# A relation layer's row-fetching matmuls cut into seven pieces and dealt out between the thin stages of a step

## The chip, the cores and the metric

The kernel runs on one core of a Trainium2 chip. What counts is the device time of one launch in microseconds, the median of several runs. A separate execution is taken by the hardware profiler; its times are in the profile.

## The reference

A graph of 6250 nodes with 128 features and 200,000 edges goes through two layers of weighted neighbour means with a normalised output, a residual and a layer norm, and then through one relation layer (32 relations in 8 bases) with a residual and a layer norm. The change touches the relation layer alone:

```python
def _L1_gnn_ref(h, src, dst, etype, norm, weight, w_comp, bias_param):
    hsrc = h[src]
    coef = w_comp[etype]
    msg = jnp.zeros((hsrc.shape[0], weight.shape[2]), dtype=h.dtype)
    for b in range(weight.shape[0]):
        msg = msg + hsrc @ weight[b] * coef[:, b][:, None]
    msg = msg * norm
    node_repr = jax.ops.segment_sum(msg, dst, num_segments=h.shape[0])
    node_repr = node_repr + bias_param
    return jax.nn.relu(node_repr)

x = _layernorm(x + _L0_gnn_ref(x, edge_index, edge_weight, L0_gnn_W1, L0_gnn_b1, L0_gnn_W2, L0_gnn_b2), axis=-1)
x = _layernorm(x + _L1_gnn_ref(x, src, dst, edge_type_32, edge_weight1, L1_gnn_weight, L1_gnn_w_comp, L1_gnn_bias_param), axis=-1)
```

## The kernel before

The kernel builds a dense adjacency matrix in DRAM, streams it twice for the two layers of means, and ends with the relation layer, which fills the span from about 2080 us on. Edges come in tiles of 128, ordered by destination. The first 428 tiles are sorted again by source into 7 classes of 7 node blocks (CLASS_BLOCKS = 7), and their source rows are fetched on TensorE; the other 1140 tiles' rows are gathered by GpSimd with indirect DMAs.

The layer runs in 114 steps (STEPS), the first 112 of which (GROUPS) have a group of four sorted tiles beside ten gathered ones. All semaphores and the order of every engine are written out by hand. In step s, TensorE has these parts:

- `tiles_summed(s, i)` (L1310): five gathered tiles, each one matmul of 128 rows by 64 columns (8 bases by 8 nodes). A step has two such halves.
- `sources(i, part)` (L1284): 21 matmuls of 512 columns in bf16 that fetch the rows of four sorted tiles. Each of 7 node blocks has three (high, middle and low part of the rows), all accumulated in PSUM bank 2. SOURCE_PARTS cuts them into three parts of 9, 6 and 6. The one-hot matrix ST2 comes from VectorE (L1749). ScalarE copies bank 2 into GT (`sources_copied`, L995); the next group's first part waits for that copy (s_gc).
- `sources_turned(i)` (L1319): four transposes of GT, which ScalarE copies into G2 (`turned_copied`, L1002).
- `wide_summed(i, c)` (L1327): one matmul of 336 columns for each of the four sorted tiles, from G2 and the matrix C2 (L1741).
- `coefficients(s)` (L1266, L1270): one and three small matmuls from the relation one-hot matrices, which ScalarE makes (`relations`, L972 to L981) from relation numbers that SyncE spreads over the partitions (`types_spread`, L624 and L629). They write bank 7. ScalarE copies them into COEF (`coefficients_copied`, L989); VectorE makes the matrices C (L1728) and C2 of them.
- `block_multiplied(n)` (L1346): for a node block whose sums are complete, eight matmuls with the bases' weights into another part of bank 7. ScalarE takes the result (`block_taken`, L1021) and clears that part of the ring of sums (L1026). 46 steps have one product, or two.
- `result_transposed(m)` (L1357): for four finished node blocks. VectorE adds the residual and normalises (L1806 to L1822); SyncE stores (`stored`, L644).

VectorE adds every matmul's output to rings of sums in SBUF: L1769 for each gathered tile, L1778 for each sorted one, at positions that it loads into registers between two steps (L1753). Its order in a step is: first half's additions, matrix C of the next step, results, two wide additions, one-hot matrix of step s + 3, matrix C2, joins, two wide additions, second half's additions.

The outputs of tiles, wide matmuls, transposes and results go round a ring of six PSUM banks. UNITS lists them in the order of their making, and `unit_bank_free(n)` waits for the reader of the unit six places before.

In the kernel before, TensorE's order in step s is: tiles, first half; sources of s + 2, part 0; two wide matmuls; sources, part 1; products; two wide matmuls; tiles, second half; sources, part 2; coefficients of s + 2; transposes of s + 1; results. ScalarE's is: products and results taken; copies of the fetched rows of s + 2, of the coefficients of s + 2, of the transposes of s + 1; relations of s + 3.

SyncE issues the loads for step s in one loop, and waits in it for a result's normalisation before it stores the result.

Of the kernel before, what the change touches and what calls it, by code (L numbers as in the profile page):

```python
# [44 lines left out]
CLASSES = 7  # L45
# [43 lines left out]
UNIT_BANKS = [0, 1, 3, 4, 5, 6]  # L89
RING_BANKS = len(UNIT_BANKS)  # L90
KEPT_CHUNK = 10
SOURCE_PARTS = [(0, 3), (3, 5), (5, CLASS_BLOCKS)]


def sorted_begun(r):
# [71 lines left out]
for step in range(STEPS):  # L167
    if step == 0:
        UNITS.append((0, "turn", 0))
    UNITS.append((step, "tile", 0))  # L170
    if step < GROUPS:
        UNITS += [(step, "wide", i) for i in range(PER)]
    UNITS.append((step, "tile", 1))
    if step + 1 < GROUPS:
        UNITS.append((step + 1, "turn", 0))
    UNITS += [(step, "result", m) for m in range(len(OUT_AT)) if OUT_AT[m] == step]
UNITS += [(step, "result", m) for step in range(STEPS, OUT_AT[-1] + 1) for m in range(len(OUT_AT)) if OUT_AT[m] == step]
UNIT = {u: n for n, u in enumerate(UNITS)}
# [57 lines left out]
def regular(nc, flag, x, src, dst, etype, w, w1, lin1, b1, lin2, b2, Wrel, wcomp, brel, out):  # L236
    with ExitStack() as ctx:
# [563 lines left out]
        def _(act):  # L801
# [242 lines left out]
            for s in range(OUT_AT[-1] + 3):  # L1044
                if KEPT_CHUNK + s < len(CHUNKS):
                    halved(KEPT_CHUNK + s)
                for n in events_in(s - 1):
                    block_taken(n)
                for m in range(len(OUT_ORDER)):
                    if OUT_AT[m] == s - 1:  # L1050
                        rooted(m)
                if s + 2 < GROUPS:
                    sources_copied(s + 2)
                if s + 2 < STEPS:
                    coefficients_copied(s + 2)
                if s + 1 < GROUPS:
                    turned_copied(s + 1)
                if s + 3 < STEPS:
                    relations(s + 3)

        @block.tensor
        def _(pe):
# [195 lines left out]
            def coefficients(s):  # L1258
                pe.wait_ge(s_rel, marked_to(s))
                if s:  # L1260
                    pe.wait_ge(s_coefc, s)
                before = events_to(s - 3, lambda n: True)
                if before:
                    product_taken(before - 1)
                if s < GROUPS:
                    nc.tensor.matmul(bank(7, PER * BASES, STEP_TILES * BASES), RELT2[s % 2],  # L1266
                                     wcd[0:PER * RELS, 0:PER, :].rearrange("p a b -> p (a b)"), start=True, stop=True)
                for q in range(-(-STEP_TILES // 4)):
                    k = min(4, STEP_TILES - 4 * q)
                    last = nc.tensor.matmul(bank(7, k * BASES, q * 4 * BASES), RELT[s % 2][0:k * RELS, q * P:(q + 1) * P],  # L1270
                                            wcd[0:k * RELS, 0:k, :].rearrange("p a b -> p (a b)"), start=True, stop=True)
                last.then_inc(s_coef, 1)

            def sources(i, part):
                if part == 0:
                    pe.wait_ge(s_st2, i + 1)
                    if i:
                        pe.wait_ge(s_gc, i)
                first = group_of(i) // ROUNDS_SORTED * CLASS_BLOCKS
                begin, end = SOURCE_PARTS[part]  # L1280
                pe.wait_ge(s_low, CHUNK_OF[first + end - 1] + 1)
                for j in range(begin, end):
                    for a, rows_part in enumerate((XS[:, first + j, 0, :], XS[:, first + j, 1, :], LOW[:, first + j, :])):
                        last = nc.tensor.matmul(bank(2), rows_part, ST2[i % 2][:, j, :],  # L1284
                                                start=(j == 0 and a == 0), stop=(j == CLASS_BLOCKS - 1 and a == 2))
                if end == CLASS_BLOCKS:
                    last.then_inc(s_gs, 1)

            def unit_bank_free(n):
# [48 lines left out]
            def block_multiplied(n):  # L1338

                step, ring, b = EVENTS[n]  # L1340
                pe.wait_ge(s_addg if ring == "gathered" else s_adds, added_after(step, ring))
                pe.wait_ge(s_coefc, min(step + 3, STEPS))
                if n:
                    product_taken(n - 1)
                for a in range(BASES):
# [16 lines left out]
            coefficients(0)  # L1362
            coefficients(1)
            for i in range(2):
                for part in range(len(SOURCE_PARTS)):
                    sources(i, part)
                if i == 0:
                    sources_turned(0)
            pe.wait_ge(s_zero, 2)
            for s in range(OUT_AT[-1] + 1):  # L1370
                if s < STEPS:
                    tiles_summed(s, 0)
                if s + 2 < GROUPS:
                    sources(s + 2, 0)
                if s < GROUPS:
                    wide_summed(s, 0)
                    wide_summed(s, 1)
                if s + 2 < GROUPS:
                    sources(s + 2, 1)
                for n in events_in(s - 1):  # L1380
                    block_multiplied(n)
                if s < GROUPS:
                    wide_summed(s, 2)
                    wide_summed(s, 3)
                if s < STEPS:
                    tiles_summed(s, 1)
                if s + 2 < GROUPS:
                    sources(s + 2, 2)
                if s + 2 < STEPS:
                    coefficients(s + 2)  # L1390
                if s + 1 < GROUPS:
                    sources_turned(s + 1)
                for m in range(len(OUT_ORDER)):
                    if OUT_AT[m] == s:
                        result_transposed(m)
# [1639 lines left out]
```

## Time and profile before

| | us |
|---|---|
| median of 3 runs | 3764.12 |
| lowest and highest run | 3760.8, 3773.42 |
| span of the profiled execution | 3868.7 |

The profiled execution is another one than the three timed runs; its span goes from the first to the last instruction. On its page, TensorE's matmuls are busy for 3418.3 us (88%), VectorE for 2465.0 (64%), GpSimd for 2415.7 (62%) and ScalarE for 1351.6 (35%). The granted TensorE clock, in tenths over forty slices, is 9 in most of the first half and 8 in nearly all of the relation layer:

```profile
PEclk6999999999999999999998889888888888888897
```

In the views, PE is TensorE's matmuls, PEld its weight loads, DVE VectorE, ACT ScalarE, POOL GpSimd and SP SyncE. L1284 is line 1284 of the kernel. A float32 matmul stands as two records. The ends of matmuls are modelled, so neighbouring ones overlap, and the distance between starts is the better measure. "Remote" and "issue" as the end of a wait mean that the profile finds no instruction that ended it.

### The profile page before, as it was taken

To read this page: it belongs to the slowest core of one execution; us is meant where nothing else is said; L and a number is where in the kernel's file an instruction comes from. 1 tells how busy PE (TensorE), PEld (TensorE's weight loads), DVE (VectorE), ACT (ScalarE), POOL (GpSimd) and SP (SyncE) were. 2 spreads that over 40 slices of the span, in tenths; PEclk is the share of its full clock that TensorE was granted. 3 is DMA by queue.
4 is the path that set the end of the run, shared out by engine and by line. 5 is a ranking of instruction groups with operands and counts; after the bars stand their busy time and mean duration, and the time that the engine had idled before them with its cause. 6 is when DMAs were issued, how large, how long until landed. Compare 5 with 4: busy or idle time off the path is not lost.

```text
span 3868.7 us, 52705 instructions
## 1 busy us (share of the span) xinstructions
PE 3418.3 (88%) x17077; PEld 2281.2 (59%) x17077; DVE 2465.0 (64%) x4684; ACT 1351.6 (35%) x3452; POOL 2415.7 (62%) x2636
## 2 busy tenths in 40 slices
PE   3999999998999999999996888888988888988885
PEld 3899999984533344544443555556655556655554
DVE  7999999995776663022033666666656666666664
ACT  5999999990000000010002222222222222222221
POOL 5888888880036775555523666666666666666663
PEclk6999999999999999999998889888888888888897
DMA  6677777778779999999993222232222222222222
GB/s 185 192 206 205 206 208 208 208 205 291 263 233 256 269 259 269 301 271 275 293 298 93 65 66 70 60 78 70 70 57 71 65 74 67 73 65 69 67 66 46
DMA packets 532789, 618.45 MB, mean 160 GB/s; under 512 B 74011, under 2 KB 460127, under 8 KB 532399
## 3 DMA queue, kind: packets, MB, share of 16 engines
q1 hardware_dynamic: 478895, 528.52, 46.9%
q0 software_dynamic: 53616, 86.51, 8.9%
q8 instruction: 140, 2.29, 0.2%
q14 instruction: 138, 1.13, 0.1%
HBM read 445.83 MB, written 168.99 MB: 159 GB/s over the span
## 4 chain that ended last, share of the span: by engine, by line
PE 49%; ACT 19%; DVE 8%; issue 8%; DMA 7%; another core or an unknown queue 7%; DVEq 2%; POOL 1%; SPq 0%; ACTq 0%; POOLq 0%
PE PS L1231 21%; ACT arena L845 11%; PE PS L1284 10%; DMA arena<-adjacency 7%; ACT arena L861 6%; PE PS L1310 5%; PE PS L1327 5%; PE PS L1270 2%; PE PS L1119 2%; PE PS L1346 1%; DVE XT L1769 1%; PE PS L1319 1%; DVEq L1753 1%; DVE H L1749 1%
## 5 line engine op out<-in xcount | busy, mean ns | idle before, releaser
L797 POOL DMA_INDIRECT arena<-x_table,rec x1140 | 1159.6, 1017 | 613.0 <-issue 309.8
L776 POOL DMA_INDIRECT sorted_records<-arena x428 | 505.9, 1182 | 556.2 <-PE PS L1231 476.5
L1119 PE MATMUL PS<-arena 128*98 128x128 f32 x6272 | 761.6, 279 | 46.3 <-DVE arena L1508 13.0
L1119 PEld LDWEIGHTS PS<-arena 128*98 128x98 f32 x6272 | 708.4, 166 | 95.9 <-issue 50.4
L733 POOL TENSOR_SCALAR arena<-iota,H,arena 128x98 f32<-128x98 f32 x980 | 674.2, 702 | 91.7 <-PE PS L1119 89.2
L1284 PE MATMUL PS<-H,X 128*128 128x512 bf16 x1568 | 548.9, 436 | 74.5 <-issue 66.9
L845 ACT ACTIVATE arena<-arena 128x98 f32<-128x98 f32 x1568 | 582.9, 686 | 12.7 <-DVE arena L1506 12.6
L1231 PE MATMUL PS<-arena,X 128*128 128x512 f32 (+1 forms) x1274 | 541.4, 577 | 39.3 <-DMA arena<-adjacency 38.6
L1231 PE MATMUL PS<-arena,H 128*128 128x512 f32 (+1 forms) x1274 | 527.8, 570 | 16.0 <-DMA arena<-adjacency 15.5
L861 ACT ACTIVATE arena<-PS 98x1024 f32<-98x1024 f32 x392 | 519.6, 1325 | 12.5 <-PE PS L1119 12.5
L1769 DVE TENSOR_TENSOR XT<-XT,PS 128x64 f32 x1140 | 252.1, 221 | 421.6 <-issue 188.8
L1508 DVE TENSOR_TENSOR arena<-PS,H 128x2048 f32<-128x2048 f32 x196 | 447.0, 2280 | 0.0
L1687 DVE TENSOR_TENSOR arena<-arena 128x1536 f32<-128x1536 f32 (+1 forms) x192 | 343.9, 1791 | 157.2 <-DMA arena<-adjacency 151.5
L1231 PEld LDWEIGHTS PS<-arena,X 128*128 128x128 f32 x1274 | 237.4, 192 | 322.4 <-issue 193.3
L1231 PEld LDWEIGHTS PS<-arena,H 128*128 128x128 f32 x1274 | 238.5, 190 | 293.8 <-issue 215.3
L1310 PEld LDWEIGHTS PS<-arena 128*128 128x128 f32 x2280 | 320.6, 213 | 78.9 <-issue 46.8
L1310 PE MATMUL PS<-arena 128*128 128x64 f32 x2280 | 323.3, 292 | 46.5 <-issue 33.4
L1327 PE MATMUL PS<-arena 128*128 128x336 f32 x896 | 313.5, 472 | 43.5 <-issue 35.5
L1284 PE MATMUL PS<-H,arena 128*128 128x512 bf16 x784 | 337.6, 431 | 1.2 <-issue 1.0
L1778 DVE TENSOR_TENSOR arena<-arena,PS 128x336 f32 x448 | 224.7, 501 | 173.9 <-remote 75.7
L1284 PEld LDWEIGHTS PS<-H,X 128*128 128x128 bf16 x1568 | 172.5, 117 | 257.4 <-issue 162.9
L995 ACT ACTIVATE rec<-PS 128x512 f32<-128x512 f32 x112 | 66.7, 596 | 682.7 <-remote 439.7
(259 smaller groups left out, 3139.6 us busy)
## 6 DMA issues: line engine op xcount, KB each, us to landing
arena<-adjacency SPq DMA_DIRECT2D x294, 768.0 KB
adjacency<-arena SPq DMA_DIRECT2D x196, 784.0 KB
arena<-adjacency SPq DMA_DIRECT2D x98, 832.0 KB
arena<-x_table,rec POOLq DMA_INDIRECT x1140
XT<-sorted_source_rows SPq DMA_DIRECT2D x112, 128.0 KB
arena<-in_edge_type SPq DMA_DIRECT2D x226, 48.0 KB
arena<-in_edge_type SPq DMA_DIRECT2D x226, 32.0 KB
XT<-sorted_relations SPq DMA_DIRECT2D x448, 8.0 KB
```

The costliest lines, as they stand in the source:

```text
L733: last = nc.gpsimd.tensor_scalar(S1[:, r, :], iota[:, 0:M1], K1T[:, v:v + 1], WWT[:, v:v + 1], ALU.is_equal, ALU.mult)
L776: pool.indirect_dma_start(rec2_d, bass.IndirectOffsetOnAxis(ap=SLOT[:, t:t + 1], axis=0), R4[:, t, :], None).then_inc(s_scat, 16)
L797: pool.indirect_dma_start(G[:, n % HELD_UNITS * UNIT_TILES + i, :], None, x1_d, bass.IndirectOffsetOnAxis(ap=SRC[:, t:t + 1], axis=0)).the ...
L845: nc.scalar.activation(S1[:, r, :], S1[:, r, :], ACT.Copy, scale=WWT[:, v:v + 1]).then_inc(s_wa, 1)
L861: nc.scalar.activation(ST[0:M1, n % 3, q * GROUP * P:(q + 1) * GROUP * P], PS[0:M1, q * GROUP * P:(q + 1) * GROUP * P], ACT.Copy).then_inc ...
L1119: last = nc.tensor.matmul(bank(2 * q + j // 4, P, j % 4 * P)[0:M1, :], S1[:, r, :], S2[:, r, :], start=True, stop=True)
L1231: last = nc.tensor.matmul(bank(bank0 + c, nb * P), (X, H1)[l][:, k, :], AB[n % 4][:, off:off + nb * P], start=(k == 0), stop=(k == NBLK - 1))
L1284: last = nc.tensor.matmul(bank(2), rows_part, ST2[i % 2][:, j, :], start=(j == 0 and a == 0), stop=(j == CLASS_BLOCKS - 1 and a == 2))
L1310: last = nc.tensor.matmul(bank(UNIT_BANKS[n % RING_BANKS], BASIS, j * BASIS), G[:, half % HELD_UNITS * UNIT_TILES + j, :], C[s % 2][:, fir ...
L1327: nc.tensor.matmul(bank(UNIT_BANKS[n % RING_BANKS], WIDE_BASIS), G2[i % 2][:, c, :], C2[i % 2][:, c, :, :].rearrange("p b j -> p (b j)"), ...
L1508: nc.vector.tensor_tensor(S2[:, whole, :], bank(4, P).unsqueeze(1).to_broadcast([P, BATCH, P]), each(K2T, n).to_broadcast([P, BATCH, P]), ...
L1687: nc.vector.tensor_tensor(ACC[p % 2][:, 0:width], ACC[p % 2][:, 0:width], AB[n % 4][:, 0:width], ALU.add).then_inc(s_acc, 1)
```

## The change

TensorE fetches a group's rows in seven pieces of three matmuls, one for each node block, where it had three parts of 9, 6 and 6. In step s the order becomes: tiles, first half; piece 0; transposes of s + 1; piece 1; two wide matmuls; piece 2; coefficients of s + 2; piece 3; products; two wide matmuls; piece 4; tiles, second half; pieces 5 and 6; results.

ScalarE's order becomes: transposes of s + 1, relations of s + 3, coefficients of s + 2, products and results taken, fetched rows of s + 2.

In the list of units, the transposes stand behind the first half of tiles and no longer behind the second. Two waits follow the new order. The coefficients wait for the products up to those of four steps before their own index, instead of three. A product waits for the copy of one more step's coefficients. The wait for the low part of the rows (s_low) is made for each piece, in the first seven groups only.

```diff
-SOURCE_PARTS = [(0, 3), (3, 5), (5, CLASS_BLOCKS)]
@@
     UNITS.append((step, "tile", 0))
+    if step + 1 < GROUPS:
+        UNITS.append((step + 1, "turn", 0))
     if step < GROUPS:
         UNITS += [(step, "wide", i) for i in range(PER)]
     UNITS.append((step, "tile", 1))
-    if step + 1 < GROUPS:
-        UNITS.append((step + 1, "turn", 0))
@@ scalar
                 if KEPT_CHUNK + s < len(CHUNKS):
                     halved(KEPT_CHUNK + s)
+                if s + 1 < GROUPS:
+                    turned_copied(s + 1)
+                if s + 3 < STEPS:
+                    relations(s + 3)
+                if s + 2 < STEPS:
+                    coefficients_copied(s + 2)
                 for n in events_in(s - 1):
                     block_taken(n)
...
                 if s + 2 < GROUPS:
                     sources_copied(s + 2)
-                if s + 2 < STEPS:
-                    coefficients_copied(s + 2)
-                if s + 1 < GROUPS:
-                    turned_copied(s + 1)
-                if s + 3 < STEPS:
-                    relations(s + 3)
@@ coefficients
-                before = events_to(s - 3, lambda n: True)
+                before = events_to(s - 4, lambda n: True)
@@ sources
-            def sources(i, part):
-                if part == 0:
+            def sources(i, j):
+                first = group_of(i) // ROUNDS_SORTED * CLASS_BLOCKS
+                if j == 0:
                     pe.wait_ge(s_st2, i + 1)
                     if i:
                         pe.wait_ge(s_gc, i)
-                first = group_of(i) // ROUNDS_SORTED * CLASS_BLOCKS
-                begin, end = SOURCE_PARTS[part]
-                pe.wait_ge(s_low, CHUNK_OF[first + end - 1] + 1)
-                for j in range(begin, end):
-                    for a, rows_part in enumerate((XS[:, first + j, 0, :], XS[:, first + j, 1, :], LOW[:, first + j, :])):
-                        last = nc.tensor.matmul(bank(2), rows_part, ST2[i % 2][:, j, :],
-                                                start=(j == 0 and a == 0), stop=(j == CLASS_BLOCKS - 1 and a == 2))
-                if end == CLASS_BLOCKS:
+                if i < CLASSES:
+                    pe.wait_ge(s_low, CHUNK_OF[first + j] + 1)
+                for a, rows_part in enumerate((XS[:, first + j, 0, :], XS[:, first + j, 1, :], LOW[:, first + j, :])):
+                    last = nc.tensor.matmul(bank(2), rows_part, ST2[i % 2][:, j, :],
+                                            start=(j == 0 and a == 0), stop=(j == CLASS_BLOCKS - 1 and a == 2))
+                if j == CLASS_BLOCKS - 1:
                     last.then_inc(s_gs, 1)
@@ block_multiplied
-                pe.wait_ge(s_coefc, min(step + 3, STEPS))
+                pe.wait_ge(s_coefc, min(step + 4, STEPS))
@@ the loop over steps
+                ahead = s + 2 < GROUPS
                 if s < STEPS:
                     tiles_summed(s, 0)
-                if s + 2 < GROUPS:
+                if ahead:
                     sources(s + 2, 0)
+                if s + 1 < GROUPS:
+                    sources_turned(s + 1)
+                if ahead:
+                    sources(s + 2, 1)
                 if s < GROUPS:
                     wide_summed(s, 0)
                     wide_summed(s, 1)
-                if s + 2 < GROUPS:
-                    sources(s + 2, 1)
+                if ahead:
+                    sources(s + 2, 2)
+                if s + 2 < STEPS:
+                    coefficients(s + 2)
+                if ahead:
+                    sources(s + 2, 3)
                 for n in events_in(s - 1):
                     block_multiplied(n)
                 if s < GROUPS:
                     wide_summed(s, 2)
                     wide_summed(s, 3)
+                if ahead:
+                    sources(s + 2, 4)
                 if s < STEPS:
                     tiles_summed(s, 1)
-                if s + 2 < GROUPS:
-                    sources(s + 2, 2)
-                if s + 2 < STEPS:
-                    coefficients(s + 2)
-                if s + 1 < GROUPS:
-                    sources_turned(s + 1)
+                if ahead:
+                    sources(s + 2, 5)
+                    sources(s + 2, 6)
```

## Rows read from the trace of the kernel before

**Rows 1.** The page's first line.

```profile
span 3868.7 us, 52705 instructions
```

**Rows 2.** By windows: length, each engine's busy us and instructions, granted clock, DMA share, GB/s.

```profile
2110.00:3760.00 1650.00, 1426.03 (x7334) 972.33 (x7333) 1060.57 (x3151) 431.61 (x1067) 1091.06 (x1073) 0.87 0.26 68
```

**Rows 3.** Timeline of VectorE, step 60: start, us, line, count, idle time before.

```profile
3018.00 1.64 DVE L1769 TENSOR_TENSOR XT<-XT,PS 128x64 f32 x5 [2.79 <-issue]
...
3027.22 1.64 DVE L1769 TENSOR_TENSOR XT<-XT,PS 128x64 f32 x5
3031.06 0.93 DVE L1769 TENSOR_TENSOR XT<-XT,PS 128x64 f32 x3 [2.20 <-issue]
```

**Rows 4.** Waits of VectorE, 2110 to 3760 us: total us, times, longest.

```profile
DVE XT L1769 <- issue: 179.5, 79, 2.8
DVE arena L1778 <- remote: 72.5, 28, 6.7
...
DVE arena L1778 <- ACT arena L1026: 18.1, 7, 4.9
```

**Rows 5.** Timeline of TensorE, step 60 and the start of step 61.

```profile
3027.17 1.23 PE L1310 MATMUL PS<-arena 128*128 128x64 f32 x10
3028.23 0.59 PE L1284 MATMUL PS<-H,X 128*128 128x512 bf16 x2
...
3030.18 1.29 PE L1327 MATMUL PS<-arena 128*128 128x336 f32 x4
...
3033.73 1.22 PE L1310 MATMUL PS<-arena 128*128 128x64 f32 x10
...
3036.09 0.30 PE L1266 MATMUL PS<-wcd,XT 128*128 128x32 f32 x2
...
3037.09 0.66 PE L1319 MATMUL PS<-ident,rec 128*128 128x128 f32 x4
3037.58 0.56 PE L1310 MATMUL PS<-arena 128*128 128x64 f32 x2
```

**Rows 6.** Timeline of ScalarE, 3013 to 3019 us.

```profile
3013.63 0.60 ACT L995 ACTIVATE rec<-PS 128x512 f32<-128x512 f32 x1 [15.34 <-remote]
...
3016.49 0.51 ACT L972 ACTIVATE H<-arena,rel_of 128x256 f32<-128x256 int32 x1
...
3018.32 0.39 ACT L981 ACTIVATE XT<-XT,ones 128x128 f32<-128x128 f32 x1
```

**Rows 7.** Timeline of TensorE, 3006 to 3016 us.

```profile
3006.69 0.38 PE L1284 MATMUL PS<-H,arena 128*128 128x512 bf16 x1
...
3014.32 1.01 PE L1284 MATMUL PS<-H,X 128*128 128x512 bf16 x2 [4.70 <-issue]
...
3015.56 1.06 PE L1284 MATMUL PS<-H,X 128*128 128x512 bf16 x2
```

**Rows 8.** Waits of all engines, 2100 to 3790 us: ScalarE's longest.

```profile
ACT rec L995 <- remote: 439.7, 47, 17.9
```

**Rows 9.** By windows: a stretch of thin matmuls and the one behind it.

```profile
2157.70:2161.10 3.40, 2.74 (x21) 2.30 (x20) 3.15 (x10) 0.00 (x0) 2.49 (x4) 1.00 0.19 47
2161.10:2174.80 13.70, 7.18 (x16) 2.80 (x17) 8.00 (x24) 3.41 (x9) 9.23 (x9) 0.50 0.21 54
```

**Rows 10.** Waits of TensorE, 2110 to 3760 us.

```profile
PE PS L1266 <- ACT H L1021: 14.3, 7, 3.1
```

**Rows 11.** Timelines of TensorE and SyncE: the first and the last of nine such steps.

```profile
2514.17 1.00 PE L1310 MATMUL PS<-arena 128*128 128x64 f32 x8
2519.07 1.84 SPq L629 DMA_DIRECT2D arena<-in_edge_type  x4
...
3685.82 1.23 PE L1310 MATMUL PS<-arena 128*128 128x64 f32 x10
3692.64 1.84 SPq L629 DMA_DIRECT2D arena<-in_edge_type  x4
```

More of the change, by code:

```diff
@@ L1364, in _ @@
             for i in range(2):
-                for part in range(len(SOURCE_PARTS)):
-                    sources(i, part)
+                for j in range(CLASS_BLOCKS):
+                    sources(i, j)
                 if i == 0:
```

## The prediction

> **What bounds the kernel now.** I read the page first, then the relation stage by itself, then one step of it on each engine, and last what each engine waits for. The page gives the span [rows 1]; the change touches only its last stage. The view by windows [rows 2] has that stage's steps 0 to 106 between 2110 and 3760 us, 107 steps in 1650 us: 15.4 us a step. TensorE's granted clock is 0.87 there: it was at its lower level, 1.2 GHz, for 26% of the time (1 - 0.26/2 = 0.87).
>
> VectorE next. In a step in which it waits for nobody, its first tile addition starts at 3018.00 and that of the next step at 3031.06 [rows 3]: 13.06 us. Some 2.2 to 2.8 us of these are shown as idle "issue"; there it loads the ring positions for the next step's additions (L1753) into registers, which no engine can shorten. What VectorE loses to others is in its waits [rows 4]. The gaps ahead of L1769 are nearly all these loads (179.5 us in 79). Ahead of L1778 stand 72.5 us of waits for a late signal of TensorE and 18.1 for a ring that ScalarE clears. With the smaller groups of the same kind, and 20 us beyond the loads ahead of L1769, I count 137 us of true waits. So VectorE has (1650 - 137)/107 = 14.1 us of its own in a mean step (13.06, and about 1 for joins, wraps and the ten results).
>
> TensorE has less. Step 60 at the full clock [rows 5] runs from 3027.17 to 3037.58: 10.4 us. By its starts: five tiles 1.06; nine row-fetching matmuls 1.95 (0.65 for three); four wide ones with six fetching ones between them 3.55 (3.55 - 1.30 = 2.25, 1.13 for two); tiles and six fetching ones 2.36; coefficients 1.00; transposes 0.49. A block product (46 steps have them, four of these have two) adds about 2, so 11.4 on average at the full clock and 11.4/0.87 = 13.1 at the clock it got. That is under VectorE's 14.1. **VectorE sets the period**; TensorE runs ahead of it (tiles of step 60 at 3027.17, their addition at 3031.06: 3.9 us; in other steps up to 10) and matters only when it falls behind.
>
> **The profiled execution is longer than the others.** Its span is 3868.7 us, the median of the runs 3764.12: 104.6 less. I ask where the 105 us are, because they decide what can be gained. ScalarE, idle for 15.34 us, begins the copy of step 58's fetched rows at 3013.63 [rows 6], but the last matmul that it waits for stands at 3006.69 to 3007.07 [rows 7]: the completion was told 6.5 us late. TensorE's next fetch waits for that copy, so it starts at 3014.32, and the clock has fallen: three fetching matmuls take 1.24 us instead of 0.65. ScalarE's waits for such signals with nothing to match them come to 439.7 us in 47 of 112 copies [rows 8]. If that happens only under the profiler, about 105 of VectorE's 137 us of waits aren't there in an ordinary run, and 32 us are left for any change of TensorE's order.
> The Trainium skill (NOTIFIC — the notification-queue block, section 7.1) says that the recorder's internal pipeline holds back its producers when it is full. By that rule the late signals are the profiler's; no run here shows it, and no number below needs it.
>
> **The change part by part.**
> 1. Order. Matmuls, banks, copies are the same in number; nothing is added or removed but waits that are already met (one on s_low for each piece of the first seven groups). Counted from the step's start by the pieces of [rows 5]: tiles 0 to 1.06, piece 1.71, transposes 2.20, piece 2.85, two wide 3.98, piece 4.63, coefficients 5.63, piece 6.28, products, two wide 7.41, piece 8.06, tiles 9.12, two pieces 10.4. The same 10.4: zero.
> 2. Clock. Before, coefficients, transposes, and the next tiles lie side by side, 2.6 us with few columns. A fall is seen behind such a place: 2157.7 to 2161.1 has TensorE busy for 2.74 of 3.40 us, mostly with thin matmuls, at the full clock, and the 13.7 us after it are at 1.2 GHz [rows 9]. Spread out, no thin group but the tiles is over 1.1 us long. If half the low-clock time went (430 us of the stage's 1650, half of it lost), TensorE would gain some 105 us. It isn't on the path: VectorE's own 14.1 us hide it, and of the 32 us of waits I give it 15.
> The Trainium skill (TensorE: Matmul & The Clock Gate, "The HAM clock gate") has the clock go back to half when the engine stands idle and return with activity. That leaves open what thin work counts for, and a TensorE with 3 us to spare in 14 will stand idle somewhere in any order; by that rule this part is worth about nothing.
> 3. Coefficients. They no longer wait for the product of the same step to be taken (the bound moves from s - 3 to s - 4): L1266 <- ACT L1021, 14.3 us in 7 waits [rows 10], and the likes, 23 us in all. TensorE again, so 5 us of VectorE's waits.
> 4. Products. They now stand behind the coefficients and a piece: at 6.28 instead of 1.06 + 1.95 + 1.13 + 1.29 = 5.43, 0.85 us later. VectorE's third wide addition waits for the ring that ScalarE clears after them: 18.1 us in 7 waits [rows 4], 25 in 12 with the second ring. 12 x 0.85 = 10 us worse.
> 5. A new wait: a product writes bank 7 and must find coefficients s + 2 copied. ScalarE does this behind the transposes' copy and the relations of s + 3, six activations from 3016.49 to 3018.71 [rows 6], 2.2 us: 2.20 + 0.6 + 2.2 = 5.0, before the coefficients end at 5.63; the copy is done by 6.0, before 6.28. Zero, if the relation numbers are there. In nine steps they aren't: SyncE has just waited for a result. First such step: tiles at 2514.17, the last load issued until 2520.91; last: 3685.82 and 3694.48 [rows 11], 8.7 us into the step, and landing is later still. Then relations until 10.9, coefficients' copy until 11.2, against 6.28: TensorE stands 4.9 us or more if the step has a product (five of the nine). Queued behind: products, wide matmuls, tiles, the fetches; on ScalarE the clearing and the next copy of fetched rows. TensorE's lead of 4 to 10 us covers this; the charge is 0 at one end and 5 x 5 + 4 x 2 = 33 at the other (2 where there is no product, for the late copy of fetched rows); I take 4, as the lead is longer in most steps.
> 6. Fetched rows. The next step's first piece waits for their copy. Before, coefficients, transposes and tiles (2.55 us) lay between; now the tiles alone (1.06), against 0.38 - 0.22 + 0.60 and hops, about 0.85. Zero with 0.2 to spare at the full clock; if the signals are late in ordinary runs too, up to 1.5 us a step of TensorE, under its cover.
> 7. Banks. The ring of six now makes the second tiles wait for the first tiles' additions of the same step: ready at 3031.06 + 1.64 in step 60, 5.5 us into the step, against 8.06; where TensorE leads by 10 it waits 3.6 us. VectorE needs these tiles only 9.2 us after its first addition began (3027.22 against 3018.00), so this shortens the lead and costs nothing by itself.
> Sum: -15 - 5 + 10 + 4 = -6; with VectorE's own time untouched. Bounds: below, all 32 us; above, +15.
>
> **The rivals.**
> A. VectorE's waits are real in ordinary runs, and the steadier clock ends them. For it: late signals fit no copy's length, and nothing here proves them to be the profiler's. Then the sum is taken from 137: two fifths of it, 55, less the 10 of part 4: -45, 3719 us; at most -100.
> B. Slower: ScalarE's relations, now ahead of the coefficients and the fetched rows' copy, hold TensorE in the nine steps behind a late SyncE, just where results already eat its lead. It decides from where the lead is under 4.9 us: step 60's is 3.9. With 33 us for that, 10 for the products, less 20 gained: +23, 3787 us.
> C. It doesn't do what it says: the clock falls from idle time, not from thin work, and stays 0.87; parts 3 to 5 cancel: 3764 us.
>
> **How the numbers follow.** Forecast: VectorE-bound, a small gain, 45%: 3764.1 - 6 = 3758 us, range 3732 to 3779. A 23%, B 20%, C 12%. This kernel's measurement can tell 0.3%, 11 us, from no change. Faster: a third of the forecast (0.15) and all of A (0.23), 0.38. Slower: B (0.20) and 0.03 from the upper end of the forecast, 0.23. Same: 0.39. The range takes in most of A and B: 3700 to 3800; beyond lie a quarter of A (100 us is its most) and a fifth of B, whose signals may be late too (part 6).
>
> **What would show it.** In the profile after: DVE L1769's start to start still 13.1 us in quiet steps and 15 on average (forecast), under 14.6 (A). Clock of the stage: 0.90 or more (part 2), 0.87 (C). ACT L989 idle, ended by something late, ahead of PE L1346 in steps 27, 52, 65, 81, 91 (B). PE L1310 waiting for DVE L1769 (part 7), L1266 no more for ACT L1021 (part 3). I am wrong if VectorE's own operations get shorter in runs without the profiler, or if the first piece of a step waits for ScalarE throughout.

## The result, and the profile after

The changed kernel takes 3781.59 us (3775.89 to 3789.68, six runs), the kernel before 3764.03 in the same comparison: 17.6 us longer, ratio 1.0041, interval 1.0025 to 1.0057. I had forecast 3758 us and a small gain. The time lies in the range of 3700 to 3800, but it moved the other way, as rival B has it.

The page of the changed kernel begins with its span, which is now that of an ordinary run (its own time is 3789.68); the span of before was 105 us over its timed runs [rows 1]:

```profile
span 3787.9 us, 52562 instructions
```

The view by windows, 2110 to 3760 us (columns as in [rows 2]), has the layer's clock at 0.93. The 0.87 of before belongs to an execution with late signals, so the two can't be set against each other as they stand:

```profile
2110.00:3760.00 1650.00, 1386.89 (x7592) 973.85 (x7732) 1127.85 (x3363) 471.99 (x1156) 1185.11 (x1140) 0.93 0.30 73
```

VectorE's waits, 2110 to 3690 us (line, who ended it, total us, times, longest):

```profile
DVE XT L1775 <- issue: 130.6, 54, 2.8
DVE XT L1775 <- PE PS L1325: 120.9, 47, 3.1
DVE arena L1784 <- DVE arena L1784: 42.6, 194, 0.6
...
DVE arena L1784 <- ACT XT L1025: 6.7, 5, 2.8
DVE XT L1775 <- PE PS L1308: 5.9, 6, 1.3
DVE arena L1784 <- ACT arena L1025: 5.1, 1, 5.1
```

L1775 and L1784 are the additions that were L1769 and L1778. The first two rows are the register loads, 2.5 us each, whatever ended a wait in them; the third is VectorE behind itself. The waits for late signals, 72.5 us ahead of L1778 alone [rows 4], are gone altogether, though not by the change, as the experiments show. What is left are waits of 1 to 5 us, and they lie in six steps, found by going through the additions in order: 27 (4.2 us), 52 (1.9), 65 (1.1), 78 (3.7), 81 (1.3) and 91 (5.4), 17.6 in sum. These are the five steps with a product behind a late load that the prediction names (steps 27, 52, 65, 81, 91), and step 78, whose product I had overlooked. The trace has ten late loads, not nine; the other four, in steps 39, 45, 103 and 108, have no product behind them and cost VectorE nothing.

Step 91 shows how. SyncE, then ScalarE, TensorE and VectorE:

```profile
3445.72 0.41 SPq L643 DMA_DIRECT2D out<-H  x1
...
3448.66 1.90 SPq L628 DMA_DIRECT2D arena<-in_edge_type  x4
```

```profile
3452.86 0.51 ACT L971 ACTIVATE arena<-arena,rel_of 128x256 f32<-128x256 int32 x1 [9.16 <-DMA arena<-in_edge_type]
...
3454.98 0.24 ACT L988 ACTIVATE XT<-PS 128x112 f32<-128x112 f32 x1
```

```profile
3439.60 1.22 PE L1308 MATMUL PS<-arena 128*128 128x64 f32 x10
...
3449.40 1.10 PE L1269 MATMUL PS<-wcd,H 128*128 128x32 f32 x6
...
3455.32 3.75 PE L1344 MATMUL PS<-XT,Wr 128*128 128x128 f32 x16 [4.07 <-issue]
3459.63 3.75 PE L1344 MATMUL PS<-arena,Wr 128*128 128x128 f32 x16 [0.55 <-ACT H L1020]
```

```profile
3451.58 1.64 DVE L1775 TENSOR_TENSOR XT<-XT,PS 128x64 f32 x5 [2.81 <-issue]
...
3464.87 0.50 DVE L1784 TENSOR_TENSOR arena<-arena,PS 128x336 f32 x1 [5.13 <-ACT arena L1025]
```

SyncE stores a result at 3445.72, once VectorE has normalised it, and only then asks for the relation numbers (3448.66). ScalarE waits 9.16 us for them, makes the relations, and behind them the copy of the coefficients (L988, 3454.98), though those had been multiplied since 3450.5. The products (L1344) wait for that copy and are both slow, and the ring that ScalarE clears after them (L1025) is 5.13 us late for VectorE's third wide addition. TensorE began the step 12.0 us ahead of VectorE (3439.60 against 3451.58), and it didn't help.

Half of what a product takes here is the clock. A product that didn't have to wait takes 1.95 us, as in step 88 of the same trace; by windows (the last three numbers are granted clock, DMA share and GB/s), it has the full clock and the two of step 91 have half of it:

```profile
3403.35 1.95 PE L1344 MATMUL PS<-XT,Wr 128*128 128x128 f32 x16
```

```profile
3403.40:3405.30 1.90, 1.90 (x18) 1.90 (x17) 0.34 (x2) 0.00 (x0) 1.59 (x2) 1.00 0.29 73
3455.40:3463.30 7.90, 7.35 (x33) 7.08 (x34) 4.27 (x11) 1.31 (x2) 0.00 (x0) 0.50 0.20 49
```

All seven products of the six steps ran like this, at 0.50 and in 3.75 us each. TensorE had stood idle for 3.5 to 6.5 us before the first of each step.

### The profile page after: what moved, and what is told of

It is laid out like the page before. It is cut to its first block, busy times and chain, and to the rows that moved or that the text cites. A ratio compares the mean times of both kernels' runs of the same rounds, so it can differ in the third digit from the quotient of the medians.

```text
span 3787.9 us, 52562 instructions
## 1 busy us (share of the span) xinstructions
PE 3315.4 (88%) x16935; PEld 2226.6 (59%) x17077; DVE 2466.3 (65%) x4684; ACT 1361.5 (36%) x3452; POOL 2442.2 (64%) x2636
## 4 chain that ended last, share of the span: by engine, by line
PE 33%; DVE 21%; ACT 18%; DMA 11%; issue 9%; DVEq 7%; POOL 1%; SPq 0%; POOLq 0%; ACTq 0%
PE PS L1230 19%; ACT arena L844 11%; DMA arena<-adjacency 10%; ACT arena L860 6%; DVE XT L1775 5%; DVEq L1759 5%; DVE H L1755 5%; PE PS L1282 3%; PE PS L1325 2%; DVE arena L1784 2%; PE PS L1308 2%; PE PS L1344 2%; PE PS L1118 2%; DVEq L1775 1%; DVE arena L1734 1%
## 5 line engine op out<-in xcount | busy, mean ns | idle before, releaser
L796 POOL DMA_INDIRECT arena<-x_table,rec x1140 | 1185.1, 1040 | 458.2 <-issue 329.7
L1230 PE MATMUL PS<-arena,H 128*128 128x512 f32 (+1 forms) x1274 | 535.5, 575 | 31.2 <-DMA arena<-adjacency 30.9
L860 ACT ACTIVATE arena<-PS 98x1024 f32<-98x1024 f32 x392 | 520.2, 1327 | 12.3 <-PE PS L1118 12.3
L1775 DVE TENSOR_TENSOR XT<-XT,PS 128x64 f32 x1140 | 252.0, 221 | 407.8 <-issue 137.0
L1282 PE MATMUL PS<-H,X 128*128 128x512 bf16 x1447 | 461.6, 395 | 62.4 <-DVE H L1755 52.6
L1308 PEld LDWEIGHTS PS<-arena 128*128 128x128 f32 x2280 | 304.2, 203 | 110.4 <-DVE XT L1775 83.8
L1308 PE MATMUL PS<-arena 128*128 128x64 f32 x2280 | 301.9, 283 | 59.8 <-DVE XT L1775 58.8
L1282 PE MATMUL PS<-H,arena 128*128 128x512 bf16 x763 | 300.9, 394 | 0.4 <-issue 0.4
L1512 DVE TENSOR_TENSOR arena<-PS,H 128x1078 f32<-128x1078 f32 x196 | 250.6, 1279 | 41.4 <-PE PS L1118 34.2
L1325 PEld LDWEIGHTS PS<-arena 128*128 128x128 f32 x896 | 165.6, 199 | 185.9 <-issue 67.7
L1784 DVE TENSOR_TENSOR arena<-arena,PS 128x336 f32 x448 | 224.3, 501 | 68.7 <-DVE arena L1784 44.9
```

The lines of the kernel that those rows point to most:

```text
L796: pool.indirect_dma_start(G[:, n % HELD_UNITS * UNIT_TILES + i, :], None, x1_d, bass.IndirectOffsetOnAxis(ap=SRC[:, t:t + 1], axis=0)).the ...
L860: nc.scalar.activation(ST[0:M1, n % 3, q * GROUP * P:(q + 1) * GROUP * P], PS[0:M1, q * GROUP * P:(q + 1) * GROUP * P], ACT.Copy).then_inc ...
L1230: last = nc.tensor.matmul(bank(bank0 + c, nb * P), (X, H1)[l][:, k, :], AB[n % 4][:, off:off + nb * P], start=(k == 0), stop=(k == NBLK - 1))
L1308: last = nc.tensor.matmul(bank(UNIT_BANKS[n % RING_BANKS], BASIS, j * BASIS), G[:, half % HELD_UNITS * UNIT_TILES + j, :], C[s % 2][:, fir ...
L1325: nc.tensor.matmul(bank(UNIT_BANKS[n % RING_BANKS], WIDE_BASIS), G2[i % 2][:, c, :], C2[i % 2][:, c, :, :].rearrange("p b j -> p (b j)"), ...
L1775: nc.vector.tensor_tensor(a, a, bank(UNIT_BANKS[n % RING_BANKS], BASIS, j * BASIS).rearrange("p (b j) -> p b j", j=SPAN), ALU.add).then_in ...
```

## The experiments

Theories ahead of the first runs: 1, late relation numbers are the whole difference; 2, a small loss in every step; 3, it lies before the layer. Each edit was measured beside the kernel before on the same chip, and the comparisons turned out to be of two kinds: in some TensorE's signals come on time, in others late. So ratios and not times are to be compared. Four comparisons, on three chips, had late signals; one chip came up twice, late both times (3859.8 and 3886.2 us). The comparison at 3743.6 us, on a fourth chip, had them on time, and so has the first one, whose chip isn't on record. That it is the chip and not the moment isn't shown, though I write of chips below.

| kernel | before there, us | ratio, 95% interval |
|---|---|---|
| e5 the changed kernel | 3743.6 | 1.0035 (1.0021 to 1.0049) |
| e7 relations last | 3743.6 | 0.9993 (0.9977 to 1.0009) |
| e8 later store | 3743.6 | 0.9995 (0.9981 to 1.0010) |
| e6 before, 14 of 21 fetches | 3743.6 | 0.9992 (0.9975 to 1.0008) |
| e14 the changed kernel | 3859.8 | 1.0541 (1.0499 to 1.0582) |
| e2 relations last | 3911.8 | 1.0463 (1.0397 to 1.0528) |
| e3 later store | 3911.8 | 1.0397 (1.0337 to 1.0457) |
| e13, e15 products first | 3859.8, 3890.4 | 1.0404, 1.0379 |
| e9, e17 later store, one-hot shared | 3886.2, 3890.4 | 1.0408, 1.0430 |
| e10 before, one-hot shared | 3886.2 | 1.0037 (1.0017 to 1.0056) |
| e4, e12 before, pieces only | 3911.8, 3886.2 | 1.0049, 1.0045 |
| e18 before, 14 of 21 fetches | 3890.4 | 0.9934 (0.9903 to 0.9965) |
| e1, e11, e16 the kernel before | 3911.8, 3886.2, 3890.4 | 1.0003, 0.9986, 1.0002 |

**The kernel before again (e1, e11, e16).** No edit.

> The kernel before, unchanged, for a second profile of it. The changed kernel came out 17.6 us slower than before (3781.6 against 3764.0), and in its profile VectorE waits 17.6 us for others in six steps (27, 52, 65, 78, 81, 91) and hardly anywhere else. Theory 1 (late relation numbers: the six steps are the whole difference): the profile of the kernel before, without late signals this time, shows VectorE's first tile addition of step 0 as far from the end as 3764 less its start allows, periods that average about 14.1 us, and no wait over 1 us ahead of VectorE's wide additions in those six steps. Theory 2 (a small loss in every step, 17.6 / 112 = 0.16 us): the quiet steps of the kernel before are 0.16 us shorter than the 13.2 and 14.0 us of the changed one. Theory 3 (the difference lies before the relation layer): the first addition of step 0 comes some 18 us earlier than the 2147.4 us of the changed kernel. If the late signals of TensorE are the kernel's own, they are there again: 440 us of waits ahead of the copies of fetched rows. If they belong to that one execution, they are gone, and the span is 3762 us.

All three were on chips with late signals, and all their runs are long, not one execution: 3903.5, 3881.5 and 3888.9 us. In e1 ScalarE's copy of the fetched rows waits as in [rows 8] (waits, 2150 to 3700 us):

```profile
ACT rec L995 <- remote: 329.9, 35, 12.8
ACT H L1021 <- remote: 250.2, 24, 12.0
```

The first profile's 3868.7 us lie within the 3850 to 3925 us that the kernel before takes there. Its trace is of their kind in another way too: it holds 32,036 semaphore updates where the changed kernel's holds 61,387 (the last section has the others). There is no profile of the kernel before with signals on time, so what the change did to its waits there is read from e6, e7 and e8.

> The kernel before, for a profile of it where TensorE's signals are on time. VectorE-bound: first additions 14.08 to 14.11 us apart on average as in the changed kernel with its loads in time, own waits of VectorE for others under 20 us in the layer, no step of 27, 52, 65, 78, 81, 91 over 14.2 us. Rival: waits of 20 us or more that the change took away, and that it paid for with something else. Granted clock of the layer about 0.90, from the mean of the whole run, 0.943 against the changed kernel's 0.954. Where signals are late again: 3900 us and the waits of the first profile.

> The kernel before, for its profile. Where signals are on time: VectorE's first additions 14.08 to 14.11 us apart on average, as in the variants of the changed kernel with ratio 0.999; no step of 27, 52, 65, 78, 81, 91 over 14.3 us, save those that are long for their results (65); granted clock of the layer about 0.90 against 0.94. If the change had taken waits away and paid for it elsewhere, the average is above 14.2. Where signals are late: 1.000, as twice before.

**The changed kernel again (e5, e14).** No edit.

> The changed kernel itself, beside the kernel before. In the first experiments the kernel before took 3912 us on the chip of that study, where it had taken 3764 us on the chip of the first comparison, and TensorE's signals came up to 12 us late and in bursts, as in its first profile. So there are two kinds of chip or of moment, and the change has to be judged on each. Where the kernel before takes 3764 us and signals are on time: ratio 1.004 again, VectorE's waits in steps 27, 52, 65, 78, 81, 91. Where it takes 3900 us: the step's first fetching piece waits for a copy with 1.06 us to spare in place of 2.55, and products wait for a copy more; if that is what late signals act on, the ratio is about 1.04, as for the two variants (1.046 and 1.040); if the variants were slow by their own edits, it is 1.004 there too.

> The changed kernel itself. Where signals are late: 1.04 to 1.05, as its variants with the relations last (1.046) and the later store (1.040), with over 140 us of waits ahead of VectorE's third wide addition. Where they are on time: 1.0035 again.

On the chip with signals on time it is 13.6 us slower, with the waits in the same steps (step 91: 4.9 us). On the other it is 210 us slower, fifteen times as much. The first is explained below; the second only in part.

**Relations last (e2, e7).** ScalarE alone:

```diff
                 if s + 1 < GROUPS:
                     turned_copied(s + 1)
-                if s + 3 < STEPS:
-                    relations(s + 3)
...
                 if s + 2 < GROUPS:
                     sources_copied(s + 2)
+                if s + 3 < STEPS:
+                    relations(s + 3)
```

> The changed kernel with ScalarE's relations of s + 3 put back to the end of its step, behind the copy of the fetched rows; all else as changed. Theory 1 (relations that wait for a late load hold the coefficients' copy, and with it the products): the waits in steps 27, 52, 65, 78, 81, 91 go, and the time is that of the kernel before, 3764 us or a few less. Theory 2 (a small loss in each step): still 3780 us. Theory 3 (the difference lies before the relation layer): still 3780 us.

> The changed kernel with ScalarE's relations of s + 3 at the end of its step, once more, beside the changed kernel itself. With signals on time: 17 us less than the changed kernel, the time of the kernel before (ratio 1.000), because the products of steps 27, 52, 65, 78, 81 and 91 no longer stand behind a late load; 1.004 if each step loses a little. With late signals: 1.046 again, and within 1 per cent of the changed kernel.

Where signals are on time, the 17 us go: 3740.2 us against 3757.2 for e5. From the first addition of step 0 to that of step 113 it is 1590.9 us (2114.0 to 3704.9) where e5 has 1603.9 (2121.7 to 3725.6): 13.0 us in the layer. Of these, 12.3 us are in the six steps, and no other step differs by more than 0.5. The two profiled executions differ by another 7.7 us before the layer, where the two programs are the same; the edit has no part in those. In VectorE's waits (2140 to 3700 us) the row "ACT arena L1025" of e5 is gone:

```profile
DVE arena L1784 <- ACT arena L1025: 4.9, 1, 4.9
```

and in e7 the third wide addition of step 91 (L1784, behind L1747) stands without a wait:

```profile
3403.99 1.64 DVE L1775 TENSOR_TENSOR XT<-XT,PS 128x64 f32 x5 [2.80 <-issue]
...
3410.60 1.56 DVE L1747 TENSOR_TENSOR arena<-XT 128x1344 f32<-128x1344 f32 x1
3412.07 0.50 DVE L1784 TENSOR_TENSOR arena<-arena,PS 128x336 f32 x1
```

**Later store (e3, e8).** SyncE alone: `while OUT_AT[kept] + 6 <= s` became `+ 7`.

> The changed kernel with SyncE storing each result one round of its loop later (7 in place of 6 steps behind the result's own), so that the relation numbers of the next step are asked for before SyncE waits for the normalisation. ScalarE's order stays as changed. Theory 1: the nine late loads come one step before anybody needs them, the six waits go, 3764 us, and ScalarE's waits for the loads of relation numbers (9 us each in nine steps) are under 1 us. Theory 2 or 3: still 3780 us. If the later store delays the load of the residual of the result after the next, a few us could be lost instead.

> The changed kernel with SyncE storing results one round of its loop later, once more, beside the changed kernel itself. With signals on time: the relation numbers are there in all steps, ratio 1.000 or a little below; 1.004 if each step loses a little. With late signals: 1.040 again.

The other end of the same chain, and the same outcome: 3741.8 us. SyncE now issues the loads for step 94 before it stores, and ScalarE's copy of coefficients in step 91 begins at 3404.91, 2.6 us before VectorE's step at 3407.49; in the changed kernel it was 3.4 us after it. Two edits at different engines that share only the late load each bring the loss back to nothing. Theory 1 holds where signals are on time; 2 and 3 fall.

**Fewer fetches in the kernel before (e6, e18).** The low part of the rows is left out, 14 of 21 matmuls remain:

```diff
-enumerate((XS[:, first + j, 0, :], XS[:, first + j, 1, :], LOW[:, first + j, :]))
+enumerate((XS[:, first + j, 0, :], XS[:, first + j, 1, :]))
```

> The kernel before without the low part of the rows: 14 row-fetching matmuls a step in place of 21 (the rows are fetched less exactly). TensorE's step is 7 x 0.216 = 1.5 us shorter of 10.4, 170 us in all. If VectorE sets the period, as the prediction has it, a chip with signals on time shows the same time within 0.3 per cent. If TensorE sets it, up to 170 us less. Where signals are late: if they are late because TensorE's own work is slower than its records say, 100 us or more are gained; if the signals are held up by something else, little.

Where signals are on time, 1.5 us less of TensorE in each of 112 steps are worth nothing. TensorE only stands idle more, and its clock is lower: 0.926 over the whole run against 0.943 for the kernel before beside it. In the layer it is 0.87, where the changed kernel with the later store, which differs from it in order and in number of fetches, has 0.95 (window 2110 to 3700 us of e6, then of e8):

```profile
2110.00:3700.00 1590.00, 1322.44 (x6848) 917.19 (x6846) 1107.00 (x3279) 458.06 (x1109) 1169.38 (x1133) 0.87 0.30 74
```

```profile
2110.00:3700.00 1590.00, 1366.88 (x7623) 944.45 (x7622) 1104.83 (x3282) 457.73 (x1110) 1176.78 (x1130) 0.95 0.29 74
```

VectorE's busy time is the same in both, 1107 and 1105 us: it sets the period. In e6 it is 14.11 us (2116.7 to 3711.1 in 113 steps), in e7 14.08.

> The kernel before without the low part of the rows, 14 row-fetching matmuls a step in place of 21, once more. Where signals are on time: 0.999 again. Where they are late: if lateness comes of the matmuls' own number or time, 100 us or more less (ratio 0.97 or below); if it is a delay of the signals whatever TensorE does, 0.99 to 1.00.

Where they are late, 24 us are gained of the 170 us of TensorE work left out. So most of the time lost to late signals stays when a third of the fetches are gone.

**Pieces only (e4, e12).** The kernel before with the fetches in seven pieces and nothing else moved.

> The kernel before with the row-fetching matmuls in seven pieces, and nothing else moved: tiles, pieces 0 and 1, two wide, piece 2, products, piece 3, two wide, piece 4, tiles, piece 5, coefficients, piece 6, transposes. ScalarE's order, the list of units and the waits are those of before. Theory 1: the pieces alone neither cost nor bring anything, 3764 us within 0.3 per cent. Theory 2 (a loss in each step that comes of the pieces): between 3770 and 3782 us. If thin work side by side is what lowers the clock, the granted clock of the relation layer goes up from that of the kernel before; VectorE sets the period all the same.

Both on chips with late signals: 1.0049 and 1.0045. A small loss there; where signals are on time it wasn't measured. The clock didn't rise (0.85 against 0.86 in e1, between 2110 and 3760 us), so the split by itself doesn't keep it up, at least not there.

**Products first (e13, e15).** In the changed kernel:

```diff
-                if s + 2 < STEPS:
-                    coefficients(s + 2)
-                if ahead:
-                    sources(s + 2, 3)
                 for n in events_in(s - 1):
                     block_multiplied(n)
+                if ahead:
+                    sources(s + 2, 3)
                 if s < GROUPS:
                     wide_summed(s, 2)
                     wide_summed(s, 3)
+                if s + 2 < STEPS:
+                    coefficients(s + 2)
@@ the two waits as before; ScalarE takes products ahead of copying coefficients
```

> The changed kernel with the products put back ahead of the coefficients, on TensorE (tiles, piece 0, transposes, piece 1, two wide, piece 2, products, piece 3, two wide, coefficients, piece 4, tiles, pieces 5 and 6) and on ScalarE (transposes, relations, products taken, coefficients, fetched rows), with the two waits of the kernel before. The pieces, the early transposes and ScalarE's early relations stay. Theory P (what costs is that a product now waits for the copy of the coefficients of s + 2, made in the same step): where signals are on time, 3744 us (ratio 1.000) though the relations still wait for nine late loads; where they are late, the 142 to 173 us of VectorE's waits ahead of its third wide addition fall to the 25 us of the kernel before, ratio 1.01 or less in place of 1.04. Theory F (the fetched rows' copy, with 1.06 us to spare in place of 2.55): ratio 1.0035 and 1.04 stay.

A quarter of the loss goes (1.054 to 1.040 on one chip), the rest stays. Theory P is right on what it names: VectorE's waits for the ring that ScalarE clears fall from 170.9 us (the last two rows below) to 31.4, near the 25 it forecast. It isn't the whole. In the changed kernel (e14, waits from 2150 to 3700 us) the products and the ring stand out:

```profile
ACT XT L988 <- remote: 640.3, 81, 9.8
...
PE PS L1344 <- issue: 229.3, 33, 8.8
...
DVE arena L1784 <- ACT XT L1025: 113.6, 21, 7.1
...
DVE arena L1784 <- ACT arena L1025: 57.3, 8, 9.0
```

In e13 the waits are spread, at the coefficients' copy, at coefficients that wait for a product to be taken, and at the tiles:

```profile
ACT XT L988 <- remote: 360.9, 57, 9.8
...
DVE XT L1775 <- PE PS L1308: 90.0, 37, 3.4
...
PE PS L1265 <- ACT H L1020: 71.2, 16, 7.1
```

**One-hot shared (e9, e10, e17).** Three of the seven one-hot blocks go from VectorE to ScalarE (a square of the difference each, then one rectification, at the end of its step), with the later store in the changed kernel and without anything else in the kernel before.

> The changed kernel with SyncE storing one round later, and three of the seven one-hot blocks of a step made by ScalarE (three squares of the difference and one rectification, at the end of its step) in place of VectorE. If VectorE sets the period: 3 x 0.26 us = 0.79 us less in each of 109 steps, 86 us, ratio 0.977, as far as nothing else is next; GpSimd's ten gathers take 10 x (1.04 + 0.30) = 13.4 us a step in the profile, so it may stop at a gain of 0.7 us a step, 76 us. ScalarE, busy for 4.1 us of 14, takes about 3 us more. If TensorE or ScalarE's copies set the period after all: ratio 0.999 or above 1.

> The kernel before with the same three one-hot blocks made by ScalarE and nothing of the change. If the change's order is worth something once VectorE is lighter (its steadier clock, coefficients that don't wait for products), this one gains less than the one above, by 0.3 per cent or more. If VectorE or GpSimd sets the period in both: the same ratio as above, 0.977 to 0.980.

0.79 us a step less of VectorE bring nothing where signals are late: 1.041 and 1.043, as e3's 1.040, and 1.0037 for e10. So a lighter VectorE alone doesn't help there; as the edit also gives ScalarE 2.7 us more in each step, it doesn't tell whose time it is. Where signals are on time, where 86 us were to be expected from a bound VectorE, the kernel wasn't run. No version with the same results is shown to beat the kernel before; e18 is faster and fetches less exactly.

## Why the prediction was wrong

- **The bound** was right: VectorE's own 14.1 us a step. e7 has 14.08, and e6 takes away 1.5 us of TensorE's work a step without moving the time.
- **The profiled execution.** I took the late signals for the profiler's and left 32 of 137 us of true waits for ordinary runs. That they are absent from the timed runs of the first comparison is right. That they belong to that one execution isn't: all timed runs of e1, e11 and e16 are as long. The Trainium skill (NOTIFIC — the notification-queue block, section 7.1) says that the recorder's pipeline holds back its producers. The runs neither show nor exclude that; no run here is known to have had the recorder off.
- **Parts 1 and 7** hold: the order costs nothing by itself, and the tiles wait for VectorE (L1308 <- L1775, 58.8 us in 46 times) without cost.
- **Part 2** has two halves. The clock: on the chip with signals on time it rose, 0.954 against 0.943 over the whole run. The first 2000 us have 0.98 in every trace, so I estimate 0.90 for the layer of the kernel before there, against 0.93. Beside e14, with late signals, it fell (0.912 against 0.922), and the split alone didn't raise it, so that thin work side by side is what lowers it isn't shown; e6, which only idles more, is lower too, as rival C has it. The gain: the 15 us taken from the waits weren't there. e6, in the old order, has no wait of VectorE over 0.6 us in steps 2 to 110 beyond the register loads, so next to nothing was left to take. e7 keeps the whole order but one move, and its gain is 3.4 us, within its interval of none.
- **Part 3** likewise: coefficients no longer wait, and its 5 us weren't there. **Part 4** charged 10 us for products 0.85 us later; e7 has the products later and no such loss. **Part 6**'s slack of 0.2 us sufficed where signals are on time: the first piece waits for the one-hot matrix (L1282 <- L1755, 52.6 us in 69), not for the copy.
- **Part 5** is the step that turned the sign. It found the late loads and the path over ScalarE to the products, and priced them at 0 to 33, with 4 taken because "TensorE's lead of 4 to 10 us covers this". Measured: 17.6 and 13.6 us. Two things were wrong in it. First, the lead cannot cover the load. The load waits for a normalisation of VectorE's, so it is late by VectorE's time, however early TensorE had started: in the six steps it reaches ScalarE 0.8 to 3.2 us after VectorE's step began, 1.3 us in step 91 (3452.86 against 3451.58). I reckoned its 8.7 us from TensorE's start; in step 91 of the changed kernel, with a lead of 12.0 us, it was 13.3. Second, I priced a product at the full clock, about 2 us. The stall itself takes the clock away, and each product behind it took 3.75. From the load on, step 91 has relations 2.1, the coefficients' copy and one product 4.1, taking and clearing 1.3: 8.8 us into VectorE's step, and its third wide addition is due after 8.1 (3412.07 against 3403.99 in e7). With 1.95 for the product it would have been 7.0, in time. Worked through the six steps in this way, with 1.8 us less for each product and each step set against the same one in e7, some 7 of 18 us would be left in the first comparison and 2 of 12 in e5. This is an estimate, no run tests it; by it most of the loss is the clock behind the stall.
- **Rival B** had the mechanism and its place. Its point of decision (a lead under 4.9 us) was wrong for the same reason, and of its terms only the 33 was real, at half its size. That its 3787 us lie near the measured 3781.6 is luck: a loss of 10 and a gain of 20 that weren't there nearly make up for the rest. The sign set for rival A, additions under 14.6 us apart on average, came true (14.26) in a slower kernel; it told the absence of late signals and not a gain.

What remains open: why TensorE's signals are late on some chips, and which moves besides the products' make up the rest of the 4 to 5 per cent there.

## What to carry to other kernels

A wait that is tied to the bounding engine cannot be hidden by another engine's lead over it: count when the late event comes from the start of the bounding engine's own step. Price what stands behind a stall of TensorE at the low clock: here it made the products twice as long. Before a step is put ahead of others in an in-order queue, list what each of its inputs is waited for on, and keep anything that hangs on a rare late load last; here moving the relations back, or the store one round later, undid the loss. And where waits in a profile match nothing, find out whether the timed runs contain them before anything is priced from that trace.

## What the runs showed of the hardware

The same program takes 3744 or 3764 us in some comparisons and 3860 to 3912 us in others. Nearly all of the difference lies in the relation layer: from the first addition of step 0 to that of step 113 the five traces with signals on time have 1591 to 1611 us, the others 1729 to 1940. What differs is when TensorE's completions are told. In e14 the coefficients' matmuls are over by 2902.65, and ScalarE has nothing else to do than copy their output:

```profile
2901.72 0.93 PE L1269 MATMUL PS<-wcd,arena 128*128 128x32 f32 x6
2902.59 0.61 PE L1282 MATMUL PS<-H,X 128*128 128x512 bf16 x2
2903.03 0.38 PE L1282 MATMUL PS<-H,arena 128*128 128x512 bf16 x1
2912.15 3.76 PE L1344 MATMUL PS<-XT,Wr 128*128 128x128 f32 x16 [8.74 <-issue]
```

```profile
2911.79 0.26 ACT L988 ACTIVATE XT<-PS 128x112 f32<-128x112 f32 x1 [9.48 <-remote]
```

ScalarE learns of it 9.1 us later, and TensorE idles for 8.74 us. In another step of the same trace four signals arrive within 0.22 us (2808.48 to 2808.70), after none since 2801.24, so they look held and let go together. VectorE's and ScalarE's own signals, as far as they are recorded, come within 0.01 us of the instruction's end in every trace (98 of 100 from 2150 us on), and so do TensorE's where signals are on time. Which signal is late goes with the order. By the median, e14's coefficients are told 7.5 us late and its products in time; in e1 it is the other way round, the products 4.2 us late. That an order with more turns from TensorE to ScalarE and back is the more sensitive is my reading of this; no run tests it.

One more thing separates the two kinds. The five traces with signals on time hold 61,220 to 61,800 semaphore updates, the fifteen others, the first profile of the kernel before among them, 28,116 to 35,179, for programs of much the same number of instructions. Most of the missing ones are of the relation layer: from its first addition on e1 has 10,404, the changed kernel's first trace 38,141. So in such a trace the name of what ended a wait is often missing or a wrong one, and the starts of instructions are the safer reading. Whether the missing records and the late signals have one cause isn't shown.
